# A gate's residual moved from VectorE to ScalarE and GpSimd, with later gathers, loads and scatters in the expert stage

## What is computed

```
x = x + norm(mamba(norm(x)))        # 4 heads, state 128, causal conv of 4 taps, silu gate, + inner residual
x = x + norm(moe(norm(x)))          # 8 experts, top 2 of a softmax gate; a*sigmoid(b) @ Wo
x = x + norm(attention(norm(x)))    # groups of 32: squared relu attention + linear part, gated
x = x + norm(ffn(norm(x)))          # 384 hidden, silu(gate)*up
```

## Time and profile before

| | us |
|---|---|
| median of 3 runs | 582.27 (581.85 to 584.56) |
| the profiled execution | 578.57 |
| its span, first to last instruction | 576.8 |

### The profile page before, as it was taken

The page is one execution under the profiler, slowest core; times in us unless marked ns, Lnnn a source line. Parts: engine busy times, 40 slices in busy tenths (PEclk is TensorE's granted clock), DMA queues, the critical chain, the costliest instruction groups (busy, mean ns, idle before and its releaser), DMA issues.

```text
span 576.8 us, 11015 instructions
## 1 busy us (share of the span) xinstructions
PE 484.9 (84%) x3102; PEld 396.1 (69%) x3102; DVE 455.9 (79%) x1742; ACT 306.6 (53%) x655; POOL 310.9 (54%) x349
## 2 busy tenths in 40 slices
PE   7998998899898987678678687888888998889990
PEld 3555787697786866456555465777888897778890
DVE  3885678999898899967574467888888988799974
ACT  3767775667657562244243344565555566445531
POOL 5852553726677667657432657377787232224342
PEclk9999998999999999999798798999999999999996
DMA  7704999900000001335356764321212000000111
GB/s 192 233 2 119 286 285 285 276 6 9 20 25 15 27 11 36 91 105 173 123 166 183 218 197 147 118 56 56 73 50 63 1 2 0 2 1 20 37 38 55
DMA packets 74213, 54.87 MB, mean 95 GB/s; under 512 B 5665, under 2 KB 69665, under 8 KB 74154
## 3 DMA queue, kind: packets, MB, share of 16 engines
q1 hardware_dynamic: 69034, 41.58, 24.6%
q0 software_dynamic: 5120, 12.59, 7.5%
HBM read 19.70 MB, written 34.45 MB: 94 GB/s over the span
## 4 chain that ended last, share of the span: by engine, by line
PE 39%; issue 21%; DVE 18%; POOL 12%; ACT 5%; DMA 1%; SPq 1%; another core or an unknown queue 1%; POOLq 0%; DVEq 0%; ACTq 0%
PE ps L1907 5%; POOL z_rows L557 5%; PE ps L1909 4%; PE ps L1908 4%; POOL tails L705 2%; PE ps L2303 2%; PE ps L2369 2%; POOL work L680 2%; DVE rstats_t L1248 2%; PE ps L2228 2%; PE ps L2371 2%; DVE X L1210 1%; PE ps L2128 1%; PE ps L2394 1%; PE ps L1924 1%
## 5 line engine op out<-in xcount | busy, mean ns | idle before, releaser
L570 POOL DMA_INDIRECT shared_buf<-g_rows,back x64 | 64.1, 1001 | 37.5 <-DVE slot_g L1693 21.4
L557 POOL DMA_INDIRECT z_rows<-Z,dest x64 | 64.3, 1004 | 24.5 <-issue 16.6
L1907 PE MATMUL ps<-w_hi,ZT_hi 128*128 (+1 forms) x110 | 47.8, 435 | 18.3 <-issue 11.9
L823 ACT ACTIVATE Z<-X,shift,rstds 128x128 f32<-128x128 f32 x128 | 53.3, 484 | 11.8 <-DVE shift L1174 8.6
L1009 ACT ACTIVATE half_tanh<-ps 128x256 f32<-128x256 f32 x78 | 29.2, 384 | 53.7 <-PE ps L1909 40.7
L542 POOL TENSOR_TENSOR rstds<-vars_t,mhalf 128x4 f32<-128x4 f32 (+1 forms) x24 | 31.4, 1308 | 47.5 <-DVE vars_t L1197 24.8
L1693 DVE SCALAR_TENSOR_TENSOR slot_g<-half_tanh,ps 128x256 f32<-128x256 f32 x78 | 31.5, 416 | 29.8 <-ACT half_tanh L1009 17.5
L547 POOL TENSOR_TENSOR res_rstd<-rvar,mhalf 128x4 f32<-128x4 f32 x24 | 25.2, 1051 | 38.8 <-DVE rvar L1265 38.8
L1908 PE MATMUL ps<-w_lo,ZT_hi 128*128 (+1 forms) x110 | 41.7, 379 | 0.0
L1909 PE MATMUL ps<-w_hi,ZT_lo 128*128 (+1 forms) x110 | 41.4, 377 | 0.0
L1907 PEld LDWEIGHTS ps<-w_hi,ZT_hi 128*128 128x128 f32 x110 | 21.9, 199 | 27.5 <-issue 26.4
(11 more groups left out here) (359 smaller groups left out, 1568.3 us busy)
## 6 DMA issues: line engine op xcount, KB each, us to landing
z_rows<-zero SPq DMA_DIRECT2D x34, 512.0 KB, 6.6
g_rows<-slot_g SPq DMA_DIRECT2D x38, 256.0 KB
slot_zs<-z_rows SPq DMA_DIRECT2D x78, 64.0 KB
X<-in_x SPq DMA_DIRECT2D x4, 512.0 KB, 6.5
RES<-in_W1T SPq DMA_DIRECT2D x4, 512.0 KB, 5.6
out<-X SPq DMA_DIRECT2D x7, 256.0 KB, 2.3
z_rows<-Z,dest POOLq DMA_INDIRECT x64
shared_buf<-g_rows,back POOLq DMA_INDIRECT x64
```

Source lines behind the costliest of these rows:

```text
L557: pool.indirect_dma_start(z_rows[group(i)], bass.IndirectOffsetOnAxis(ap=dest[:, i, k, c:c + 1], axis=0), Zr[i % 4][:, c], None).then_inc( ...
L570: pool.indirect_dma_start(got[:, c, k], None, g_rows[group(i)], bass.IndirectOffsetOnAxis(ap=back[:, i, k, c:c + 1], axis=0))\
L823: act.activation(dst[:, c], X[:, i, c], ACT.Identity, bias=bias[:, c:c + 1], scale=rstd[:, c:c + 1]).then_inc(z_made, 1)
L1907: pe.matmul(dst, lh, rh, start=start, stop=False)
```

## The change

- Mamba stage: for sequences 0 to 6 `x_add` on VectorE keeps only `constant`. ScalarE scales RES in place (four activations, at 2, at the end of the step, new count `scaled`), and GpSimd adds RES to X (one instruction, at 3, at the start of the step), which now gives `x_new`. Sequence 7 stays as it was.
- Rank: TensorE's fillers run only in steps below 32; in the expert stage place 2 of a gate step comes behind the tile's `slot_h`.
- Scatters of `SCATTER_TILE` from (5, 1) on wait for up to two tiles more, and `power(1, 7)` comes one scatter earlier.
- Group 1: the first quad is loaded behind tile 35 of group 0 (was 33), the next three behind tile 38 (were 35, 37, 38); gathers wait for three tiles more; `MOE_AT` and what hangs on it come two tiles later; `power(2, 0)` goes ahead of gather 12.
- End: `lastD` of sequence 6 comes behind all statistics of sequence 7.

```diff
-        SCATTER_TILE = ((4, 2, 0), (4, 3, 2), (5, 0, 5), (5, 1, 7), (5, 2, 9), (5, 3, 11), (6, 0, 13), (6, 1, 15),
-                        (6, 2, 17), (6, 3, 19), (7, 0, 21), (7, 1, 23), (7, 2, 25), (7, 3, 27))
-        LATE_LOADS = {33: 0, 35: 1, 37: 2, 38: 3}
+        SCATTER_TILE = ((4, 2, 0), (4, 3, 2), (5, 0, 5), (5, 1, 9), (5, 2, 11), (5, 3, 13), (6, 0, 15), (6, 1, 17),
+                        (6, 2, 19), (6, 3, 20), (7, 0, 22), (7, 1, 24), (7, 2, 26), (7, 3, 28))
+        LATE_LOADS = {35: (0,), 38: (1, 2, 3)}
-        MOE_AT = (8, 10, 12, 14, 16, 18, 20, 22, 24, 26, 28, 30)
+        MOE_AT = (10, 12, 14, 16, 18, 20, 22, 24, 26, 28, 30, 32)
@@ SyncE
                     if g == 0 and j in LATE_LOADS:
-                        load_quad(QUADS.index((1, LATE_LOADS[j])))
+                        for late in LATE_LOADS[j]:
+                            load_quad(QUADS.index((1, late)))
@@ GpSimd, gate
+                    if place == 0 and at == 3 and i < SEQS - 1:
+                        pool.wait_ge(scaled, (i + 1) * CH)
+                        pool.tensor_tensor(X[:, i], X[:, i], RES[:, i], ALU.add).then_inc(x_new, 1)
@@ GpSimd, expert stage
-                if (i, c) == (5, 1):
+                if (i, c) == (5, 0):
                     power(1, SEQS - 1)
             for t in range(4 * CH):
-                pool.wait_ge(g_made, GTILES[0] + 2 * t + 2)
+                if t == 12:
+                    power(2, 0)
+                pool.wait_ge(g_made, GTILES[0] + 2 * t + 5)
                 gather(t)
                 if t == 9:
                     res_power(2, 0)
-                if t == 12:
-                    power(2, 0)
@@ ScalarE, gate; and gate(i * CH + c, 1) at the end of stepA
+                    if place == 1 and at == 2 and i < SEQS - 1:
+                        act.wait_ge(rpow_made, i + 1)
+                        for c in range(CH):
+                            act.activation(RES[:, i, c], RES[:, i, c], ACT.Identity, scale=res_rstd[:, i, c:c + 1])\
+                               .then_inc(scaled, 1)
@@ VectorE, x_add
                 dve.wait_ge(rpow_made, n + 1)
+                if stage == 1 and i < SEQS - 1:
+                    constant(stage, i)
+                    return
@@ VectorE, end
                     dve.bn_stats(rstats_t[:, c], RES[:, i, c]).then_inc(rstats_made, 1)
-                if half == 0:
-                    lastD(SEQS - 2)
             rbn_aggr(4, i)
+            lastD(SEQS - 2)
@@ TensorE, gate
-                        for k in range(5):
-                            pe.matmul(bank(2)[:, 3 * P:4 * P], ident[:], ident[:], start=True, stop=True)
+                        if step < NT:
+                            for k in range(5):
+                                pe.matmul(bank(2)[:, 3 * P:4 * P], ident[:], ident[:], start=True, stop=True)
@@ TensorE, tiles
-                        elif j > 2:
-                            gate(NT + j // 2 - 1, 2)
                     slot_h(GFIRST[g] + j, n, j, experts[j - 4 * q])
+                    if g == 0 and 2 < j and j % 2 == 1 and NT + j // 2 - 1 < GATE_END:
+                        gate(NT + j // 2 - 1, 2)
...
```

More of the change, by code:

```diff
@@ L268, in build @@
         xs_made, ladd_made, x_final = sem("xs_made"), sem("ladd_made"), sem("x_final")
-        last_shift, ladd_act = sem("last_shift"), sem("ladd_act")
+        last_shift, ladd_act, scaled = sem("last_shift"), sem("ladd_act"), sem("scaled")
         taps_made, conv2_made = sem("A_taps"), sem("A_conv2")
@@ L967, in stepA @@
                         set_of(ACT.Exp)
+                gate(i * CH + c, 1)
                 if i == 1 and c == 2:
@@ L1035, in _ @@
                         accT_copy(MOE_AT.index(j - 2), 6)
-                    if g == 1 and j == 30:
+                    if g == 1 and j == 32:
                         z(2, 0)
@@ L1743, in _ @@
                         residB_tile(MOE_AT.index(j - 5))
-                    if g == 1 and j in (20, 28):
-                        rbn_stats(2, (j - 20) // 8)
-                    if g == 1 and j in (21, 29):
-                        rbn_aggr(2, (j - 21) // 8)
-                    if g == 1 and j in (24, 33):
-                        x_add(2, (j - 24) // 9)
-                    if g == 1 and j == 25:
+                    if g == 1 and j in (22, 30):
+                        rbn_stats(2, (j - 22) // 8)
+                    if g == 1 and j in (23, 31):
+                        rbn_aggr(2, (j - 23) // 8)
+                    if g == 1 and j in (26, 35):
+                        x_add(2, (j - 26) // 9)
+                    if g == 1 and j == 27:
                         bn_stats(2, 0)
-                    if g == 1 and j == 26:
+                    if g == 1 and j == 28:
                         bn_aggr(2, 0)
-                    if g == 1 and j == 29:
+                    if g == 1 and j == 31:
                         scales(2, 0)
```

## The result

The changed kernel took 589.09 us (median of four, 588.81 to 595.77), the kernel before beside it 583.17 us. The ratio is 1.0165, 95% interval 1.0122 to 1.0208, that is 9.6 us slower (7.1 to 12.1). The two medians lie 5.9 us apart, less than that interval's lower end; what follows goes by the ratio. The profiled execution of the changed kernel took 588.81 us with a span of 587.0, where before had 578.57 and 576.8. In the changed kernel's file the lines have moved: GpSimd's power L542 is L543, its gating product L705 is L709, VectorE's statistics L1186 are L1196, its scales L1172 are L1182, TensorE's transposition of slot_zs L2115 is L2128.

A forecast was written before the change was run, and what follows sets the result against it. The prediction took the loop through GpSimd's queue, not VectorE's busy time, to bound the Mamba stage. Its terms, +3.9 - 2.2 + 3.9 + 0.7 - 1.5 - 1.3, gave +3.5 us, a median of 585.8 us, range 577 to 593.

The forecast's parts named there:

- the fourth rival: Mamba stage: GpSimd's adds block VectorE in each of seven sequences, 592.8 us, half of it (589) likelier; chance 0.15.
- two credits: Expected gains: -2.2 us from TensorE's fillers and rank, -1.5 us from spacing out group 1's gathers.
- What bounds the kernel: Mamba stage: a closing loop through GpSimd's queue and VectorE's scales sets the pace; the removed additions lie mostly under TensorE's work.
- (1): Mamba stage, sequences 0 to 6: GpSimd's residual add behind four scatters delays the loop, +3.9 us, bounds 0 to 9.0.
- (2) and (5): Last sequences: fillers gone and rank moved, -2.2 us; scatters later by up to two tiles, 0.
- (3): Border of expert groups: later loads make TensorE wait, first load +1.1, second 2.8, sum +3.9 us, bounds 0 and +6.
- the clock's share: Border of expert groups: a second pause of TensorE lowers the granted clock again, +0.7 us, bounds 0 and +2.
- The third rival: Border of expert groups: the moved loads don't matter, the second is there in time, 582.3 us; chance 0.10.
- (4): Expert group 1: later gathers and combinations spread the burst of four gathers, -1.5 us, bounds -5.8 and +3.
- The second rival: Expert group 1: TensorE's pauses go with the gathers' burst, 581.5 us; chance 0.20.
- (6): Kernel's end: sequence 6's last product no longer splits sequence 7's statistics, -1.3 us, bounds -2.3 and 0.

The follow-up runs named there:

- the small add: Kernel before with the residual's move alone, GpSimd's add cut to 8 of 512 columns, the other columns' residual left out: 1.0018, 1.0 us slower.
- part 1: Kernel before with the residual's move alone (ScalarE scales RES, GpSimd adds it to X): 1.012, 7.0 us slower.
- part 3: Kernel before with only the loads of group 1's first quads moved later, behind tiles 35 and 38: 1.0069, 4.0 us slower.
- parts 2 and 5: Kernel before without fillers from step 32 on, rank behind the tile's matmuls, scatters up to two tiles later: 1.003, 1.7 us slower.
- part 6 alone: Kernel before with only sequence 6's last product moved behind the statistics of sequence 7: 1.000.
- part 4: Kernel before with gathers three tiles later, combinations two tiles later, and powers and next-stage statistics shifted with them: 0.9996.
- the early loads: Kernel before with the four late loads earlier, behind tiles 31, 33, 35 and 38 instead of 33, 35, 37 and 38: 0.9995.
- the fillers: Kernel before with only TensorE's fillers of the last three sequences taken out, rank and scatters left in place: 1.0012.
- parts 2 to 6: Changed kernel with the residual's move undone, against the kernel before: 1.0131, 7.3 us slower.
- the third group: Runs sharing a chip with the kernel before at 557.84 us: changed kernel again, loads put back, fillers removed, early loads with the new end.
- the kernel without part 3: Changed kernel with group 1's loads put back to tiles 33, 35, 37 and 38, against the kernel before: 1.0142, 7.9 us slower.
- the second group: Runs sharing a chip with the kernel before at 556.74 us: 8-column add, new end alone, earlier loads, changed kernel without the residual's move.

## Why the prediction came out as it did

The sign was right, and the time lay in the range (577 to 593), but the sum was +3.5 us and the loss 9.6 (8.4 the second time). That 589.09 stands where the fourth rival had its half price (589) is luck: that price was 3.5 us of blocks, and the runs show one block of 1.5 us and two credits, 3.7 us together, that didn't come. By its steps:

**What bounds the kernel** was right for sequences 3 and 4, where the distance grows by the add's own time: the closing loop through GpSimd and not VectorE's busy time. The run with the small add shows that VectorE's relief alone wins nothing.

**(1) The residual, +3.9 forecast, about +4.6 measured.** The clean measure is power 1 to power 5: 104.72 to 104.82 us in four traces with the whole add, 100.05 to 100.34 in ten without it. Sequences 3 and 4, forecast 1.29 each, cost 1.25 and 1.23; sequence 5, forecast 0.9, cost 0.70, though by another way: VectorE, held in its table work, comes 0.5 us later to the statistics that the power waits for. The prediction set the add's 1.29 us against 1.60 for VectorE, but those are four instructions of another kind; one TENSOR_TENSOR of 128x512 (Edec, L1605, with one input in PSUM) takes VectorE 0.68. Mis-sized was sequence 2: I took 0, since GpSimd idles 1.41 us there. That idle time was VectorE's own path, and the add stopped VectorE for 1.6 us in it. The price stood among my rivals at 1.0 for each sequence; it came in one of the three with nothing in front of the add, at 1.5. I had also missed that the trace of before shows such a hold on the same instruction, beside a two-input instruction of GpSimd that splits weights:

```profile
101.94 1.82 POOL L722 TENSOR_TENSOR wff_lo<-wffn,wff_hi 128x768 fp32r<-128x768 f32 x1
...
102.44 1.60 DVE L1600 TENSOR_TENSOR wdtx<-dtx,etail_t 128x256 f32<-128x256 f32 x1
```

wdtx ends 0.28 us behind GpSimd here too (104.04, 103.76). The Trainium skill states the block in the Mode Summary that the prediction cites, and its page SBUF — State Buffer (section SBUF: two separate sides) has the form that fits better: a VectorE operation with two SBUF inputs and a GpSimd one that reads SBUF take the shared ports in turn, each for its whole length. wdtx has two such inputs; the trace agrees in the length of the hold, but wdtx's record starts 0.47 us ahead of the add's and it was VectorE that waited, where the page says that whoever starts first has the ports.
For power 5 to power 7 I had 0.4. After shows +2.10, but three kernels without the add show as much (39.5 to 42.2 in all twelve), so I put none of it on the residual. Two things move there: the power of sequence 7 itself, and the low stretch of the clock at 220 to 260 us. All thirteen other traces have one or more, and the profiled kernel before is the only one without; that execution is also 2.6 us under the median of its kernel on that chip (578.57 against 581.15). What the stretch costs there isn't shown. In the same way the 1.71 us that after gains before power 1 is a low stretch of before at 92 to 98 us that after doesn't have. That isn't the edit's doing either: before and part 1, part 3, parts 2 and 5 and part 6 alone have the stretch and reach power 1 at 123.6 to 123.8 us; after, its repetition, part 4, the small add, the early loads and the fillers don't, and reach it at 121.8 to 122.1. (The three others have low stretches elsewhere ahead of power 1, parts 2 to 6 beside this one, and reach it at 123.5, 124.7 and 128.8.)

**(2) and (5) Ranks and scatters, -2.2 and 0 forecast.** This step failed. The fillers alone change nothing (1.0012), and with rank and scatters it is +1.7 (-0.3 to +3.9). Without them TensorE waits for the picks instead. In the run without fillers its waits at the three ranks are 0.41, 2.18 and 1.30 us, in that of part 6, which has them, none, 0.97 and none. The last two, run without fillers:

```profile
267.78 0.18 PE L1944 MATMUL ps<-pickb,earlier 128*128 128x32 bf16 x1 [2.18 <-DVE pickb L1297]
...
277.46 0.18 PE L1944 MATMUL ps<-pickb,earlier 128*128 128x32 bf16 x1 [1.30 <-DVE pickb L1297]
```

I counted as won the time in which TensorE ran fillers (3 x 1.27 = 3.8 us), but it was waiting for VectorE's picks in it: 2.9 us of it came back as waits. The +1.7 itself isn't told from nothing.
"The last scatter ends before SyncE asks for it" doesn't hold on the two later chips: there SyncE's first load stands 1.7 to 1.8 us behind the last scatter's end in every kernel with the moved scatters, and 1.7 to 3.3 in those where they weren't moved. What it costs is small. Counted from the first transposition, the last scatter ends at 54.9 to 55.5 us where it was moved and at 53.3 to 54.6 where not, but the first quad of group 1 begins at 60.0 to 60.5 against 59.6 to 62.0: no later, as far as these traces tell.

**(3) The loads, +4.6 with the clock's share.** Forecast as waits of about 4 and 3 us; after has 3.60 and 1.84, part 3 alone 3.79 and 2.05. Timed alone +4.0 (2.0 to 6.0), by the expert stage of the third group +5.0 (94.93 less 89.93) or, from the first transposition, +5.2. The size was right, its shares not quite: the first load's +1.1 isn't there in that group, where the scatters hold it; the second's stall is 2.9 (forecast 2.8); and the third, which I had keep up, costs 1.2 more, since its transfers stand in one row of twelve (6.75 us) behind the second's. The third rival falls.

**(4) Gathers, -1.5 forecast, 0.0 measured** (-2.1 to +1.6). The second rival, that the pauses go with the burst, falls: spaced out, the gathers won nothing, and on another chip the same burst runs without a pause.

**(6) The end, -1.3 forecast**, 1.46 at its place; not to be told in the timed runs.

**The sum again**, with what was measured: the residual +4.6, the loads +5.2, the end -1.5, and for parts 2, 4 and 5 together +0.5 (from the first transposition 115.39 us in the kernel without part 3, against 114.9, the mean of five kernels of the last two groups: four have none of these parts, one the fillers' alone): +8.8. The two changed kernels lost 9.6 and 8.4. The +0.5 can't be told from nothing, since those five kernels lie between 113.2 and 117.1. So the forecast's error of about 5 us is for the most part the two credits, -2.2 and -1.5, that weren't there; the residual and the loads add 0.7 and 0.6.

**What stays open.** The residual alone timed at 7.0 (3.8 to 10.1), and the other five parts at 7.3 (5.3 to 9.2), which is more than 9.6 together. The traces give 4.6, which lies within its interval, and 4.2, which lies below its own. Some of the 7.3 may lie ahead of what these parts change: their trace has a low stretch of the clock at 106 to 112 us, as no other has, and reaches the first transposition at 238.83 us, where the other three of its group do at 236.08, 236.37 and 238.41. From there on it is 4.5 us longer than their mean, less 1.5 for the end. Whether the timed runs are late in the same way isn't recorded, and no run shows that the parts don't overlap.

## What to carry to other kernels

Before moving work to a less busy engine, find its place in that engine's queue and what is behind it: here 1.3 us of it counted in full in the two sequences where four scatters stood ahead and the loop closed behind them, and the relieved engine won nothing, as it waited for TensorE. An idle stretch of GpSimd is not free for it if VectorE is on the path in it: a GpSimd operation on SBUF can hold VectorE for its length. And a filler or a gap is only worth its time if what follows it was ready; a load that waits for scatters doesn't come sooner by an earlier place in its queue. Measure a stretch between marks that the change doesn't move: the power of sequence 7, which it moves by one scatter, made parts 2, 4 and 5 look 1.8 us dearer (2.3 counted from it, 0.5 from the unmoved mark).

## What I had not expected of the hardware

- The same code took 581 us on the first chip and 557 on the two others. Of the 24 us, 17 to 20 lie in the expert stage (106.82 us in the run of part 1, 86.74 and 89.42 in the second group, all with the expert stage of before). The traces of the first group and of before have a stop of about 5 us between 274 and 287 us. In before TensorE is idle 4.78 us before 279.58, VectorE and ScalarE are idle about 2.5 us twice, and GpSimd goes on with its scatters. After has two such stops there, TensorE idle 2.51 and 3.78. All six have further pauses of TensorE of 2 to 6 between 318 and 347; the traces on the other chips have neither. The instruction queues moved the same number of packets in before and after, 26 and 33. What causes the stops isn't shown.
- Where the granted clock falls is partly chance: it fell at 92 to 98 us in some traces and not in others, whatever the edit, 1.7 us each time, and somewhere in 220 to 260 us in all but one. A single profile can make an edit look 2 us better or worse at a place that it doesn't touch.
